# Second cross attention: which engine reads a freshly projected key first

## What is computed

```python
x = x + _L1_xattn_ref(_layernorm(x, axis=-1), ctx_2048, ...)

# in _L1_xattn_ref: g = 8 key heads, hpg = 2 query heads to each, d = 128
def _ln(x, w, b):
    mu = jnp.mean(x, axis=-1, keepdims=True)
    var = jnp.mean(jnp.square(x - mu), axis=-1, keepdims=True)
    return (x - mu) * jax.lax.rsqrt(var + EPS) * w + b
...
qx = _fp8_linear_pertensor(ln_out, wqx, wqx_scale, qx_in_scale).reshape(b, s, g, hpg, d)
qx = _ln(qx, qxln_w, qxln_b)
kvx = jnp.einsum('bsi,oi->bso', cond, w_kv_x)
kx, vx = jnp.split(kvx, 2, axis=-1)
kx = _ln(kx.reshape(b, sc, g, d), kxln_w, kxln_b)
vx = vx.reshape(b, sc, g, d)
xout = _gqa(qx, kx, vx).reshape(b, s, nh * d)
```

## Time and profile before

| | us |
|---|---|
| median of 3 runs | 3686.31 |
| lowest, highest | 3679.96, 3687.12 |
| the profiled execution | 3681.27 |
| its span, first to last instruction | 3679.5 |

### The profile page before, as it was taken

The page is one execution under the profiler, slowest core; times in us unless marked ns, Lnnn a source line. Parts: engine busy times, 40 slices in busy tenths (PEclk is TensorE's granted clock), DMA queues, the critical chain, the costliest instruction groups (busy, mean ns, idle before and its releaser), DMA issues. The chain is left out here.

```text
span 3679.5 us, 75523 instructions
## 1 busy us (share of the span) xinstructions
PE 3373.0 (92%) x25760; PEld 2261.3 (61%) x25760; DVE 2266.2 (62%) x5629; ACT 1870.3 (51%) x5129; POOL 77.7 (2%) x132
## 2 busy tenths in 40 slices
PE   7999999999998989978886899999999999987799
PEld 4666666666662335556674567667667676665555
DVE  4555555555552227668886677777777777767732
ACT  5656556566544653345563554554554555534421
POOL 0000000000000000000000000000000000000000
PEclk9999999999998999999998999999999999998899
DMA  4111111111112020000002111111111111101000
GB/s 137 52 43 51 43 43 51 43 52 50 45 36 75 1 97 34 11 3 6 6 4 87 39 41 44 36 44 44 36 46 44 36 44 43 38 30 49 1 9 14
DMA packets 117807, 147.98 MB, mean 40 GB/s; under 512 B 11968, under 2 KB 95552, under 8 KB 116032
## 3 DMA queue, kind: packets, MB, share of 16 engines
q1 hardware_dynamic: 117696, 146.54, 12.5%
HBM read 138.91 MB, written 7.60 MB: 40 GB/s over the span
## 5 line engine op out<-in xcount | busy, mean ns | idle before, releaser
L436 PE MATMUL x_Kb<-x_cT,x_wk 128*128 128x257 f32 x3072 | 766.8, 384 | 15.7 <-ACT x_sq L698 8.5
L436 PEld LDWEIGHTS x_Kb<-x_cT,x_wk 128*128 128x128 f32 x3072 | 554.5, 191 | 172.7 <-issue 83.7
L473 PE MATMUL x_PC<-x_pT,x_cn 128*128 128x512 f32 x1024 | 475.1, 607 | 4.1 <-DVE x_oT L1012 0.8
L718 ACT ACTIVATE x_pr<-x_pr,x_ntop 128x257 f32<-128x257 f32 x512 | 261.1, 510 | 298.3 <-DVE x_ntop L968 157.6
L698 ACT ACTIVATE x_sq<-x_Kb 128x257 f32<-128x257 f32 x512 | 195.3, 382 | 311.3 <-DVE x_kT L951 305.7
L473 PEld LDWEIGHTS x_PC<-x_pT,x_cn 128*128 128x128 f32 x1024 | 185.0, 191 | 244.0 <-issue 242.0
L951 DVE TENSOR_SCALAR x_kT<-x_Kb,x_vecs 128x257 f32<-128x257 f32 x512 | 245.7, 483 | 75.2 <-PE x_Kb L436 68.8
L455 PE MATMUL x_Sb<-x_kT,x_qT 128*32 128x257 f32 (+1 forms) x4096 | 275.7, 383 | 4.9 <-DVE x_pr L971 3.3
L724 ACT ACTIVATE x_pr<-x_pr,x_rps 128x257 f32<-128x257 f32 x512 | 240.3, 499 | 41.1 <-DVE x_rps L981 40.8
L988 DVE COPY x_pT<-x_PTb 128x512 f32<-128x512 f32 x256 | 176.8, 691 | 119.4 <-PE x_PTb L465 117.4
L1002 DVE SCALAR_TENSOR_TENSOR x_pcT<-x_last,x_cT,x_PC 128x512 f32<-128x512 f32 x256 | 190.3, 745 | 85.4 <-PE x_PC L473 81.2
(11 more groups left out here) (313 smaller groups left out, 5966.1 us busy)
## 6 DMA issues: line engine op xcount, KB each, us to landing
x_cT<-in_ctxT SPq DMA_DIRECT2D x128, 257.0 KB, 2.8
x_cn<-in_ctx SPq DMA_DIRECT2D x128, 256.0 KB, 3.0
x_last<-x_last_row SPq DMA_DIRECT2D x128, 256.0 KB, 3.8
e_w<-in_e_w SPq DMA_DIRECT2D x3, 1152.0 KB, 7.8
c_staged_heads<-in_c_wqk SPq DMA_DIRECT2D x2, 1536.0 KB, 9.7
x_wq<-in_x_wq SPq DMA_DIRECT2D x1, 2048.0 KB, 8.1
x_wo<-in_x_wo SPq DMA_DIRECT2D x1, 2048.0 KB, 13.3
x_last_row<-x_last_rows SPq DMA_DIRECT2D x128, 2.0 KB
```

Source lines behind the costliest of these rows:

```text
L436: m = pe.matmul(Kb[j % 2][:, 0:SE], wk[:, c, g * HD:(g + 1) * HD], cT[:, b, c, :], start=c == 0, stop=c == HC - 1)
L473: m = pe.matmul(PC[h][:, :], cn[:, b, c, h * P:(h + 1) * P], pT[:, c, :], start=c == 0, stop=c == KC - 1)
L718: act.activation(pr[:, v, :], pr[:, v, :], ACT.Exp, bias=ntop[:, u:u + 1], scale=1.0 if L1 else -1.0, accum_out=ps[:, u:u + 1]).then_inc(e ...
```

## The change

Three waits are exchanged, in the second cross attention alone. ScalarE's square waits for the projected key itself (`k_done`) instead of VectorE's copy. VectorE's copy waits for the square (`k_sq`) instead of the projected key. TensorE waits for the copy (`k_raw`) before it writes the bank again, instead of the square. No instruction is added, removed or moved on any engine; the line numbers behind the first edit grow by one.

```diff
@@ project_key (TensorE)
-                pe.wait_ge(k_sq.sem, k_sq.after(t, j - 1))
+                last_reader = k_raw if L1 else k_sq
+                pe.wait_ge(last_reader.sem, last_reader.after(t, j - 1))
@@ key (ScalarE)
                 if L1:
-                    act.wait_ge(k_raw.sem, k_raw.now(t, j + 1))
+                    act.wait_ge(k_done.sem, k_done.now(t, j + 1))
                     act.activation(sq[:, g % SQ, :], Kb[j % 2][:, 0:SE], ACT.Square).then_inc(k_sq.sem, 1)
                     return
@@ copy_key (VectorE)
                 j = b * G + g
-                dve.wait_ge(k_done.sem, k_done.now(t, j + 1))
+                dve.wait_ge(k_sq.sem, k_sq.now(t, j + 1))
                 dve.wait_ge(s_done.sem, s_done.after(t, UNITS * (b - 1) + J * (g // 4 + 1)))
```

## The result

| | before | after |
|---|---|---|
| median us | 3683.14 (4 runs) | 3736.64 (4 runs) |
| lowest, highest | 3677.60, 3687.12 | 3733.37, 3739.14 |
| the profiled execution | 3681.27 | 3733.37 |
| its span | 3679.5 | 3731.6 |

The ratio is 1.0146, with a 95% interval of 1.0128 to 1.0164. The change costs 53.5 us; 3748 was forecast, within 3710 to 3795.

What follows compares the result with a forecast made beforehand. TensorE, busy 75.56 of 79.37 us per tile, was taken to set the pace. Slot terms of 4.14 us per tile made 63 us, 3744 against the profiled execution, plus 5 for the median: 3748 us, range 3710 to 3795.

Steps and rivals of the forecast that it cites:

- Which wait counts: Second cross attention: TensorE sets the pace; ScalarE's 305.7 us wait is no target; key 7's square waits for ScalarE's queue.
- The hold at key 5: Second half of every slot: key 5's copy waits behind ScalarE's exponential, 1.03 us later in slot 0, 0.99 in others.
- Slot 0: Late second query copy (L933) holds TensorE's L473: +2.28 us; shift 0 +0.73, second sum of squares +1.40.
- Slot 1: Key 7's square +0.61 us, scores behind the copy of key 7 +0.67; the first half on time.
- Slot 2: Entry +0.24 us, taken between bounds 0 and 1.1; TensorE's transpose behind the first L944 +0.71.
- Slot 3: Exponential of unit 1 +0.99 us, partly taken up by ScalarE's idle time; square of key 7 +0.18, scores +0.24.
- The sum: 4.14 us per tile; 62 us over fifteen tiles plus 1 for the last, together 63 us.
- The clock: TensorE's longest new wait, in slot 0, at most 2.6 us and split in two, costs no clock.
- The rival of the clock: Slot 0 waits add to 3.5 us and lower the clock: 1.5 us more per tile, 3770 us; 5%.
- Absorbed: Rival: VectorE's slack swallows the delay on L933 and L944, leaving 15 to 19 us, 3703 us; 14%.
- Ping-pong: Rival: delay carried from slot to slot, 8.3 us per tile in all, 3811 us, half the addition 3780; 16%.
- Faster: Rival: early squares win in slots 0 and 2 if key 5's hold is under 0.5 us: 3670 us; 3%.

Runs made afterwards that it cites:

- key 6 run: Exchange kept for key 6 of each slot only, all other keys as in the kernel before: 3660.53 us, ratio 0.9939 to the kernel before.
- key 5 alone: Exchange kept for key 5 of each slot only, all other keys as in the kernel before: 3767.36 us, ratio 1.0235 to the kernel before.
- key 5 in slot 0 alone: Exchange kept for key 5 of slot 0 only, all other keys as in the kernel before: 3715.94 us, measured once.

## Why the prediction was right

Point by point, by its own steps. Shifts are taken from the start of the tile, against the rows of after shown above.

- **Which wait counts.** Right. ScalarE's 305.7 us were no source of gain. That key 7's square waited for ScalarE's own queue is borne out by the key 6 run: shortening that queue is what moved TensorE.
- **The hold at key 5.** 1.03 and 0.99 us were forecast. VectorE's idle time there is 0.94 in every slot, and the two exponentials of slot 0 start 2.09 us apart, 1.04 more than before. Shown to be the cause by two runs from opposite sides: alone it makes the whole loss (3.96 us per tile), without it the runs show none (0.36 per tile is left).
- **Slot 0.** 2.28 forecast; L474 starts 17.14 us into the tile instead of 14.95, +2.19. Within it two errors partly cancelled. Shift 0 was only 0.47 late and not 0.73, since part of its 0.37 us of waiting before was for the norms and could be used up; so the square of key 7 was 0.20 less late than I said. And L474 started 0.23 after the query copy ended, where I had taken 0.13.
- **Slot 1.** 0.67 forecast, 0.60 at the sum of squares and 0.66 at the scores behind it.
- **Slot 2.** The entry was +0.26 (0.24 forecast). That it came so close is luck: 0.24 was picked between bounds of 0 and 1.1 without a working. The transposes behind L944 were sized wrong: 0.71 forecast, 0.43 at the first transpose (2825.91 in the row above) and 0.49 at the work behind it. Shift 0 gained 0.45 there, not 0.2: it follows the second L1057 without a pause, where I had left it a gap. This is the one term that was clearly mis-sized: 0.22 of the 0.31 us between 4.14 and 3.83 per tile.
- **Slot 3.** 0.24 forecast, 0.22 measured.
- **The sum.** 63 us forecast, 53.5 measured. 3.83 times 15, and 1 for the last tile, is 58; the profiled after has 57 in the stage, less the 5 us by which the stage began earlier. I do not know what that start depends on; it differs from one profiled execution to the next (2027.1 with key 5 alone, whose part ahead of the stage is the same). Up to about 1360 us the profiled executions of before and after lie within 1.3 us of each other; from there to 2015 us the mean granted clock was 0.93 before and 0.94 after. That the difference of the medians, 53.5, is also below 58 was not explained; the four runs of each kernel scatter by 9.5 and 5.8 us.
- **The clock.** Right for this kernel: its longest waits in the steady tiles, 1.72 and 1.62 us, came with a clock of 1.00 throughout. My bound for slot 0 was 2.6 us. The sum of squares came 1.20 later, but the matmuls ahead of it came 0.68 later too, since key 7 was held by the copy of key 5 (0.40 us idle in the row above), and 1.72 was left. In the runs of key 5 alone, with waits of 1.99 to 2.02 us, the lower level appeared in most tiles. My reason, that a wait must pass 1.83 us, was too simple all the same. With key 5 exchanged in all slots it appeared behind nine of twelve waits in slot 1 and none of twelve in slot 0; the kernel after itself kept its clock behind a wait of 2.50 us (at 2038.97, its first tile), and the key 6 run behind one of 3.44. The length of the wait alone does not decide, and what else does stays open. The rival of the clock held 5% here and was the true course in the neighbouring kernel: 1.5 us per tile was its price, 1.65 was measured, behind a single wait and not behind several that add up. The Trainium skill, "TensorE: Matmul & The Clock Gate", section "Why this matters for your kernels", warns of idle gaps between bursts of matmuls, and the gap that it names is longer than 2.0 us. Page and measurement differ, and the measurement decides: 2.0 us already brought the lower level here, in nine of twelve tiles, and 3.44 us once did not.
- **The other rivals.** "Absorbed" fell: L934 and L945 did carry the delay to TensorE (11.5 us on the page for the first). "Ping-pong" fell: the delay is taken up in each first half, and the tiles keep one length. "Faster" fell at the point it named: the hold was 0.94 to 1.03 us, not under 0.5.

## What to carry to other kernels

Two engines that read the same buffer can go in either order, and the second inherits the queue of the first: ask for each place what stands ahead of the read on the engine that goes first, and what stands behind it on the one that goes second. Here the same exchange cost 4 us a tile at the key whose square stood behind an exponential that itself waited for VectorE, and gained 1.2 us at the next key, where the squaring engine stood idle. A large wait on an engine that is half free is no target; the small wait on the engine that sets the pace is, and it named the square to hurry.

## What the runs showed of the hardware

An idle time of TensorE of 1.99 to 2.01 us was followed by a fall of the granted clock from 2.4 to 1.2 GHz in nine of twelve tiles, and that cost 1.65 us, while 1.72 and 1.83 us were not. One such wait in a tile was enough (key 5 in slot 0 alone). It was not sure to do it: with key 5 exchanged in all slots, twelve waits of 2.00 to 2.02 us in slot 0 left the clock at 2.4 GHz while nine of twelve in slot 1 did not, and single waits of 2.50 us (the kernel after) and 3.44 us (key 6 alone) left it there too. So these runs give no length above which the clock always falls. A wait a little longer than the ones already there can cost nearly as much again as it lasts, which no row of the kernel before could tell.
